# Eight-head attention layers: low parts of keys and queries taken from PSUM by VectorE, high parts rounded from PSUM by ScalarE

## The reference, cut to what matters

```python
xn = group_norm(xf) * w + b
qkv = einsum('oc,bct->bot', qkv_w, xn) + qkv_b
q, k, v = split(qkv.reshape(B * 8, 96, T), 3, axis=1)
weight = softmax(einsum('bct,bcs->bts', q * ch ** -0.25, k * ch ** -0.25), axis=-1)
a = einsum('bts,bcs->bct', weight, v).reshape(B, C, T)
h = einsum('oc,bct->bot', proj_w, a) + proj_b
return x_or_xn + h
```

## Time and profile before

| | |
|---|---|
| three runs | 1807.4, 1812.68, 1812.93 us |
| profiled execution, its time | 1806.44 us |
| its span, first to last instruction | 1804.6 us |
| eight-head part of the span | from about 555 us on |
| busy: TensorE, VectorE, ScalarE, GpSimd | 1640.8, 1048.2, 904.0, 993.7 us |
| mean granted TensorE clock | 0.956 |

### The profile page before, as it was taken

One profiled execution on the slowest core, in us unless ns is written; L12 is line 12 of the kernel. 1 busy time (PEld: TensorE's weight loads), 2 busy tenths in 40 slices (PEclk: granted clock), 3 DMA queues, 4 the chain that ended last, 5 costly groups with the idle time before them and its releaser, 6 DMA issues.

```text
span 1804.6 us, 25016 instructions
## 1 busy us (share of the span) xinstructions
PE 1640.8 (91%) x8222; PEld 1007.3 (56%) x8222; DVE 1048.2 (58%) x1643; ACT 904.0 (50%) x1488; POOL 993.7 (55%) x393
## 2 busy tenths in 40 slices
PE   4888969999993889998999999999999999999987
PEld 3767758888882454545545545555455454554532
DVE  3655645454432766765667565666676576756621
ACT  3444324334322156555665556556565566555653
POOL 1222312122103166886688677787688678767885
PEclk7999989999996689999999999999999999999999
DMA  4000000000000333031130330302303123033000
GB/s 144 19 18 18 1 1 1 1 1 1 1 0 24 70 71 69 3 71 31 42 72 1 71 73 16 71 19 59 71 1 72 42 55 71 1 96 72 1 25 24
DMA packets 25005, 67.57 MB, mean 37 GB/s; under 512 B 7200, under 2 KB 8992, under 8 KB 24864
## 3 DMA queue, kind: packets, MB, share of 16 engines
q1 hardware_dynamic: 24864, 65.78, 15.0%
HBM read 7.82 MB, written 4.19 MB: 7 GB/s over the span
## 4 chain that ended last, share of the span: by engine, by line
PE 48%; DVE 8%; issue 5%; POOL 4%; DMA 2%; ACT 1%; SPq 1%; POOLq 0%; DVEq 0%; ACTq 0%
PE psO L894 12%; PE psD L79 11%; PE psD L962 10%; PE psA L987 7%; DVE BNS L1040 6%; PE psD L906 5%; POOL PA L1218 3%; PE psO L987 3%; DMA QS<-MROW 2%; ACT PR L1151 1%; DVE sums_turned L1017 1%; DVE A L1021 1%; SPq L1242 0%; SPq L1244 0%; DVE A L1023 0%
## 5 line engine op out<-in xcount | busy, mean ns | idle before, releaser
L1040 DVE TENSOR_REDUCE BNS<-psD 128x1 f32<-128x512 f32 x1024 | 631.4, 683 | 193.2 <-PE psD L962 193.2
L1218 POOL TENSOR_TENSOR PA<-PA,PR 128x2048 f32<-128x2048 f32 x128 | 586.1, 4579 | 13.9 <-ACT PR L1151 1.7
L1151 ACT ACTIVATE PR<-psA 128x512 f32<-128x512 f32 x688 | 396.1, 607 | 329.5 <-PE psA L987 286.9
L962 PE MATMUL psD<-KS,QS 96*128 96x512 f32 x1024 | 421.3, 445 | 17.4 <-DMA QS<-SL 10.8
L987 PE MATMUL psA<-QS,KS 97*128 97x512 f32 x688 | 295.4, 438 | 38.9 <-DMA QS<-MROW 17.4
L962 PEld LDWEIGHTS psD<-KS,QS 96*128 96x128 f32 x1024 | 199.2, 195 | 139.4 <-DVE BNS L1040 92.2
L1151 ACT ACTIVATE PR<-psO 128x512 f32<-128x512 f32 x336 | 203.7, 606 | 139.2 <-PE psO L987 136.9
L609 POOL TENSOR_SCALAR P<-P,RS 128x1024 f32<-128x1024 f32 x64 | 72.1, 1126 | 365.1 <-DVE RS L348 365.1
L894 PE MATMUL psO<-PR,V 128*32 128x512 f32 x2048 | 246.5, 598 | 0.0
L1218 POOL TENSOR_TENSOR PA<-PR 128x2048 f32<-128x2048 f32 x32 | 146.4, 4576 | 149.0 <-PE psD L962 130.5
L987 PEld LDWEIGHTS psA<-QS,KS 97*128 97x128 f32 x688 | 128.7, 190 | 178.1 <-issue 93.8
(11 more groups left out here) (141 smaller groups left out, 2079.0 us busy)
## 6 DMA issues: line engine op xcount, KB each, us to landing
KS<-SH SPq DMA_DIRECT2D x128, 128.0 KB, 2.4
QS<-SH SPq DMA_DIRECT2D x128, 128.0 KB, 2.5
KS<-SL SPq DMA_DIRECT2D x64, 128.0 KB, 2.5
QS<-SL SPq DMA_DIRECT2D x64, 128.0 KB, 2.5
X<-x SPq DMA_DIRECT2D x4, 1024.0 KB, 7.9
out<-X SPq DMA_DIRECT2D x4, 1024.0 KB, 4.6
KH<-KL SPq DMA_DIRECT2D x8, 128.0 KB, 2.3
QH<-KL SPq DMA_DIRECT2D x8, 128.0 KB, 2.4
```

The lines of the kernel that those rows point to most:

```text
L962: mm = e.matmul(full, QS[0:STACK, g, q, tile * PART:(tile + 1) * PART], KS[0:STACK, g, q, h * HALF:(h + 1) * HALF], start=True, stop=True)
L1040: top = e.tensor_reduce(MXH[:, h, q, tile:tile + 1], full, AX.X, ALU.max)
L1151: e.activation(PR[:, J % 4, (s % QUADH) * HALF:(s % QUADH + 1) * HALF], score_bank(s, p), ACT.Exp, scale=scale).then_inc(exp_done, 1)
L1218: e.tensor_tensor(PA[:, :], PR[:, (J - 1) % 4, :] if j == 1 else PA[:, :], PR[:, J % 4, :], ALU.add).then_inc(sum_done, 1)
```

## The change

ScalarE reads the K and Q halves (and k, q of the prologue) from PSUM and writes them rounded into SH at once; the 128x1024 copy and its drain are gone. VectorE reads the same PSUM half again, adds the bias and subtracts SH, and writes the low part into SL. Its place in VectorE's order is the unit's due step plus LOW_LAG = 1.7. A K or Q bank counts as given back when VectorE's low part is done. GpSimd's `low` is gone, and SyncE waits for VectorE's count instead of low_done. The diff, cut to its core:

```diff
@@ -691,6 +691,7 @@
         XN_AT = 12
+        LOW_LAG = 1.7
@@ -736,7 +737,17 @@
         def taken(units, k, engine):
-            return sum((u in "vwkqKQ") == (engine == "scalar") for u, _, _ in units[:k])
+            return sum((u in "vw") == (engine == "scalar") for u, _, _ in units[:k])
+
+        def vector_order(units):
+            return sorted((at + LOW_LAG * (u in "kqKQ"), k) for k, (u, at, _) in enumerate(units) if u not in "vw")
+
+        def given_back(place, r, k):
+            if UNITS[place][k][0] in "vw":
+                return "scalar", base_of("scalar", place, r) + taken(UNITS[place], k + 1, "scalar")
+            return "vector", base_of("vector", place, r) + [j for _, j in vector_order(UNITS[place])].index(k) + 1
...
+        def keys_split(G):
+            M, u = (0, "q") if G == 0 else (G - 1, "Q")
+            place, r = (M, None) if M < 2 else (2 + M % 2, M // 2 - 1)
+            last = max(k for k, x in enumerate(UNITS[place]) if x[0] == u)
+            return given_back(place, r, last)[1]
...
-                    def all_taken(place, r, k):
-                        engine = "scalar" if k > 0 and UNITS[place][k - 1][0] in "vwkqKQ" else "vector"
-                        count = min(k, 0) + taken(UNITS[place], max(k, 0), engine)
-                        wait(e, act_free if engine == "scalar" else vec_free, base_of(engine, place, r) + count)
+                    def bank_free(place, r, k):
+                        if k < 0:
+                            wait(e, vec_free, base_of("vector", place, r) + k + 1)
+                            return
+                        engine, count = given_back(place, r, k)
+                        wait(e, act_free if engine == "scalar" else vec_free, count)
...
                         if place or k >= BANKS:
-                            all_taken(place, r, k - BANKS + 1)
+                            bank_free(place, r, k - BANKS)
...
                         elif u == "z":
                             take_half(full, p ^ i, i)
+                        elif u in "kqKQ":
+                            group, gg = (G + 1, 1 - g) if u in "KQ" else (G, g)
+                            which, mv = int(u in "qQ"), slice(i * HALF, (i + 1) * HALF)
+                            e.wait_ge(high_done, 4 * group + 2 * which + i + 1)
+                            bias = par(f"bqk{layers[1]}", 4)[:, 2 * gg + which:2 * gg + which + 1]
+                            e.scalar_tensor_tensor(out=SL[:, which, mv].bitcast(F32R), in0=full, scalar=bias, in1=SH[:, which, mv],
+                                                   op0=ALU.add, op1=ALU.subtract).then_inc(vec_free, 1)
...
-                        if what == "high":
-                            e.drain()
-                            e.activation(SH[:, which, :].bitcast(F32R), SL[:, which, :], ACT.Copy).then_inc(high_done, 1)
-                            return
...
+                                e.activation(SH[:, which, mv].bitcast(F32R), full, ACT.Identity, bias=bias).then_inc(high_done, 1)
...
-                    def low(group, which):
-                        wait(e, high_done, group * 2 + which + 1)
-                        e.tensor_tensor(SL[:, which, :].bitcast(F32R), SL[:, which, :], SH[:, which, :],
-                                        ALU.subtract).then_inc(low_done, 1)
...
-                        e.wait_ge(low_done, 2 * (G + 1))
+                        e.wait_ge(vec_free, keys_split(G))
```

More of the change, by code:

```diff
@@ L868, in eight_heads_in @@
             xn_done, xh_done, xl_done = sem("xn_done" + n), sem("xh_done" + n), sem("xl_done" + n)
-            high_done, low_done, row_dma = sem("qk_high" + n), sem("qk_low" + n), sem("max_row_filled" + n)
+            high_done, row_dma = sem("qk_high" + n), sem("max_row_filled" + n)
             stack_dma = [sem(f"stack_filled{n}_head{q}") for q in range(QUADH)]
@@ L953, in unit @@
                             halves_v = [j for j, (name, _, _) in enumerate(UNITS[place]) if name == "v"]
-                            all_taken(place, r, halves_v[i] + 1)
+                            bank_free(place, r, halves_v[i])
                             for n in range(NT // 2):
@@ L964, in unit @@
                         elif u == "T":
-                            all_taken(place, r, k)
+                            bank_free(place, r, k - 1)
                             mm = e.transpose(full[0:QUADH * NT, 0:PART], MX[:, :], ident[:, :])
@@ L1055, in phase @@
                     def phase(P, p, G, g, place, r, layers, proj=None, norm=None, norm_b=None):
-                        events = [(at, 0, k, "unit") for k, (u, at, i) in enumerate(UNITS[place])
-                                  if u not in "vwkqKQ"]
+                        events = [(at, 0, k, "unit") for at, k in vector_order(UNITS[place])]
                         if norm is not None:
@@ L1112, in run @@
                                 stacks_filled(e, G)
[L1113 to L1116, removed]
+                            if u == "v":
+                                e.activation(VT[:, mv], full, ACT.Identity,
+                                             bias=par(f"bv{layers[0]}", 2)[:, g:g + 1]).then_inc(act_free, 1)
+                            else:
+                                bias = par(f"bqk{layers[1]}", 4)[:, 2 * gg + which:2 * gg + which + 1]
+                                e.activation(SH[:, which, mv].bitcast(F32R), full, ACT.Identity, bias=bias).then_inc(high_done, 1)
                     def phase(P, p, G, g, place, r, layers, proj=None, norm=None, norm_b=None):
@@ L1122, in phase @@
                                 step = -int(-at // 1) + 1
-                                if P is not None:
-                                    assert -int(-UNITS[place][k + BANKS][1] // 1) >= step
                                 events.append((step, 0, "unit", k))
-                                if i == 1 and u in "kqKQ":
-                                    events.append((step + 1 if P is not None else step, 1, "high", k))
                         if norm is not None:
@@ L1205, in phase @@
                             input_low(norm, norm_b, layers[2])
-                            for which in range(4):
-                                low(which // 2, which % 2)
                             return
@@ L1225, in phase @@
                                                     ALU.subtract).then_inc(w3_split, 1)
-                            if G is not None and h == 0:
-                                for which in range(2):
-                                    low(G + 1, which)
                     all_phases(e, phase)
```

## The result

The changed kernel is slower. Its median is 1868.85 us against 1809.14 us of the kernel before, five runs each; the ratio is 1.0327, 95% interval 1.0304 to 1.035. The forecast was 1876 us, range 1843 to 1904.

What follows compares the result with a forecast made beforehand. TensorE's order of issue, dense from K0 to the sums, was taken as the bound. 1806.4 - 3.3 (prologue) + 69.6 (stalls) = 1872.7 us; half of the profiled execution's 6.2 us below the median added gives 1876 us, range 1843 to 1904.

Steps and rivals of the forecast that it cites:

- the stalls: Four waits of TensorE for VectorE's low parts, 4.64 us in each of 15 phases, 69.6 us in all.
- the prologue: Before the phases: first stack DMA 7.8 us earlier, 4.5 us lost again at K1 and Q1, net gain 3.3 us.
- m31: TensorE's unit m with i = 31, ahead of the sums: waits for K0's low part, stall 0.60 us.
- m33: TensorE's unit m with i = 33, ahead of the sums: waits for K1's low part, stall 0.59 us.
- m35: TensorE's unit m with i = 35, ahead of the sums: waits for Q0's low part, stall 1.84 us.
- m37: TensorE's unit m with i = 37, last before the sums: waits for Q1's low part, stall 1.61 us.
- the last link: In each stall's chain, from the end of VectorE's operation to TensorE's matmul: 0.28 us.
- The other links: Rest of the stall's chain: matmul start to VectorE's reading 0.44 us, a maximum 0.61, a low part 0.75.
- The lower bound of the low part: Shortest length allowed for VectorE's low-part operation: 0.61 us, the maximum's spacing; 0.75 us was taken.
- (a): Rival in the phases: stalls hidden, relief of ScalarE not; up to 32 us back plus 3 in the prologue; 6%.
- (b): Rival ahead of the sums: half-hidden, chain costs what the freed engines give, 1803 to 1815 us; 6%.
- (c): Rival on TensorE: the clock falls too through the stalls in each phase, 30 us more, 1903 us; 8%.

Runs made afterwards that it cites:

- e1: Changed kernel with LOW_LAG 1.4 in place of 1.7, nothing else; 1823.49 us, ratio 1.0085 to the kernel before.
- e0_changed: A further single execution of the changed kernel itself, nothing altered, taken for its profile; 1864.22 us.
- e3: Kernel before, with ScalarE rounding K and Q from PSUM, its copy and GpSimd's subtraction deleted, low parts left out; 1799.16 us, ratio 0.9956.
- e5: Changed kernel with only Q0's low part moved earlier (lag 1.4), the other three at 1.7; 1848.71 us, ratio 1.0233 to the kernel before.
- e4: Changed kernel with LOW_LAG 0.9 and ScalarE's two key halves one step earlier in the phases; 1812.34 us, ratio 1.0034 to the kernel before.
- e6: Kernel before with the change made in the prologue alone (lag 0.9), phases left as before; 1805.51 us, ratio 0.999.
- e7: Early-keys version (lag 0.9) plus five unread matmuls at each phase's start; 1815.95 us, ratio 1.0048 to the kernel before.
- e8: Prologue-only version (lag 0.9) plus five unread matmuls at each phase's start; 1810.46 us, ratio 1.0018 to the kernel before.

## Why the prediction was right

**The mechanism** was the forecast's: the bank of a K or Q half is given back behind a unit that TensorE issued just before, and TensorE stands for a chain through VectorE. e1 changes the order alone and takes 41 us of 58 with it. VectorE's gaps were long enough for the work and the order did not fit them, both as read from the rows of before.

**The size.** The sum was 69.6 us for the stalls and -3.3 for the prologue; measured are 61.7 and -3.9. Stall by stall, from the distances between the same units in the two traces: m31 0.36 (forecast 0.60), m33 0.46 (0.59), m35 1.60 (1.84), m37 1.37 (1.61), and 0.29 us in three small steps behind re-started matmuls that I had not counted; 4.08 in place of 4.64 us. The mis-sized term is the last link. I gave VectorE's end to TensorE's matmul 0.28 us: 0.05 to the weight load and 0.23 for the load ahead of the matmul. The trace has the low part's end at 747.96 and the matmul at 748.01, 0.05 us: the matmul's row begins with its load's. The trace of before had this too, behind a wait for ScalarE:

```profile
752.33 0.19 PEld L987 LDWEIGHTS psA<-QS,KS 97*128 97x128 f32 x1 [0.66 <-ACT PR L1151]
752.33 0.50 PE L987 MATMUL psA<-QS,KS 97*128 97x512 f32 x1 [0.21 <-ACT PR L1151]
```

The other links came out as taken: 0.44, 0.61, and 0.74 us for the low part in place of 0.75. The lower bound of the low part, 0.61, and the estimate of 0.66 from the Trainium skill (VectorE: DVE Perf Modes, section on the TRN2 errata) were both further off than the nearest row of the same kind.

**The median.** The sum for the profiled execution, 1872.7 us, was 8.5 us above the 1864.22 of e0_changed: 7.9 us in the phases and 0.6 us in the prologue. The last link alone is 0.24 us too much in three chains, 15 times, so 10.8 us, and m33 is 0.13 us too high; the three small steps that I had not counted take 4.4 us off again. I added 3.1 us because the profiled execution of before lay below its runs. The five-run median of before is 1809.14, not 1812.68, so it lay 2.7 us below; e0_changed lies 4.6 us below the median of its kernel. So of the 8.5 us the forecast kept 7.

**Costed at nothing.** ScalarE's copy and GpSimd's subtraction in the phases: e3 shows no gain, as forecast. The new wait of SyncE: first stack DMA at 579.73, forecast 579.7, a gain of 7.8 us; of it 3.9 us were lost again at the K and Q halves of the prologue, forecast 4.5.

**Rivals.** (a) fell with e3; (b) needed slack ahead of the sums, and the stretch grew by the whole of the stalls; (c), the clock falling through the stalls, did not happen in the stretch, at 1.00 with 12.51 of 15.53 us busy. The clock does fall at another place, the start of a phase: 1.72 us idle and then 0.50 in this kernel's phase at 777, against 1.33 us and 1.00 before; that phase is 6.0 us longer where the mean is 4.1, so it cost about 2 us. I had set (c) aside because waits at the start of a phase left the clock at 1.00 in the stretches that I read. Those stretches lie in the middle of phases and could not show it: behind two such waits of the kernel before, of 1.14 us (ending at 1144.63) and 1.22 us (at 1288.69), the clock is 0.50. That the falls evened out over the changed run, 0.959 against 0.956 mean clock and 0.99 from 704 to 1782 us in both traces, is in part luck: e5, with fewer stalls, has 0.97 there.

## What to carry to other kernels

When a second reader is put on a buffer, write down both engines' orders around it and ask which unit each must have finished before the buffer comes back: if the unit just issued is among them, the producer is serialized, however idle the new reader is. An engine's free time says whether work fits; only the order says what it costs, and moving VectorE's entries by 0.3 steps, which changed the place of two of them, was worth 41 us here. Taking work off engines that wait anyway gave nothing in 15 phases and 7 us in the one place, the prologue, where they were in line.

## What the runs showed that I had not expected

The same wait at the start of a phase costs the clock in one phase and not in another. Idle times of 1.14 and 1.22 us were followed by about 3.4 us at half of the clock (0.50, the level of 1.2 GHz) in the kernel before, and one of 1.71 us in e4, while 1.33 us in the kernel before and 1.87 us in e4 were not; behind the stalls of 1.88 us between weight loads in the middle of the phase it stayed at 1.00. The Trainium skill (TensorE: Matmul & The Clock Gate, Part 1) has the throttled state as the default that activity releases. The traces of the kernel before and of the changed kernel agree in so far as every fall in a phase stands within 1 us of the end of an idle time of 1.1 us or more; the length of the idle time alone doesn't tell which of them is followed by one, and what does stays open.

In two or three phases of the versions with low parts on VectorE this wait is 0.4 us longer than in the same phases of e3 or the kernel before (e6 has one such phase too); why stays open. And where a loop goes back to its head, three times in a run, TensorE had no instruction for 3.3 to 3.9 us in all kernels, but for 7.0 to 7.4 us at two of the three places in e7 and e8, with a few matmuls added ahead of the first wait; what the matmuls hold up there was not tried.
